# A feed-forward product of seven blocks instead of eight, in a three-product tower of layers

## The reference, cut to what matters

```python
h = s4_kernel(log_dt, x, B, inv_A_real, A_imag, 1024)      # (32, 128, 1024)
h = h + layernorm(h) @ attn_w.T + attn_b                   # 1024 x 1024
n = layernorm(h)
gates = softmax(n @ Wr.T) * 2.0                            # 4 experts
base = n @ W.T + b                                         # 1024 x 1024
lora = sum_e gates[e] * ((n @ A[e].T) @ Bm[e].T)           # rank 8 each
h = h + base + lora
```

## Time and profile before

| what | value |
|---|---|
| median of 3 runs (lowest, highest) | 809.19 us (808.93, 809.88) |
| the profiled execution: span from first to last instruction | 805.8 us |
| PE busy | 769.3 us, 95% |
| DVE busy | 622.0 us, 77% |
| ACT busy | 527.3 us, 65% |
| POOL busy | 5.5 us, 1% |
| granted TensorE clock, mean | 0.994 |
| DMA bytes | 74.65 MB |

### The profile page before, as it was taken

One profiled execution on the slowest core, in us unless ns is written; L12 is line 12 of the kernel. 1 busy time (PEld: TensorE's weight loads), 2 busy tenths in 40 slices (PEclk: granted clock), 3 DMA queues, 4 the chain that ended last, 5 costly groups with the idle time before them and its releaser, 6 DMA issues.

```text
span 805.8 us, 14896 instructions
## 1 busy us (share of the span) xinstructions
PE 769.3 (95%) x5334; PEld 377.3 (47%) x5334; DVE 622.0 (77%) x1229; ACT 527.3 (65%) x881; POOL 5.5 (1%) x22
## 2 busy tenths in 40 slices
PE   2759899999999999999999999999999999999997
PEld 1634344444444444444444444444444444444443
DVE  7899978777777787787878877777887778777532
ACT  6778876667676766766677576667766676765210
POOL 2000000000000000000000000000000000000000
PEclk9988999999999999999999999999999999999999
DMA  7869942434343333334333342434324333433323
GB/s 287 295 123 173 153 81 55 98 67 86 80 95 62 70 80 78 78 75 99 80 67 71 67 98 55 99 80 83 70 57 95 70 83 80 93 61 71 57 53 81
DMA packets 196109, 74.65 MB, mean 93 GB/s; under 512 B 184496, under 2 KB 189488, under 8 KB 195960
## 3 DMA queue, kind: packets, MB, share of 16 engines
q1 hardware_dynamic: 195992, 74.26, 42.8%
q10 hardware_dynamic: 96, 0.13, 0.0%
HBM read 14.06 MB, written 16.78 MB: 38 GB/s over the span
## 4 chain that ended last, share of the span: by engine, by line
PE 86%; DVE 4%; SPq 4%; ACT 2%; DMA 2%; issue 1%; ACTq 0%
PE ps_g L531 39%; PE ps_g L591 37%; PE ps_a L522 5%; PE ps_g L597 2%; PE ps_g L697 1%; PE ps_p L579 1%; SPq L378 1%; SPq L361 1%; DMA x<-in_L_attn_weight 1%; DVE wa_lo L1238 1%; DMA x<-x_tok 1%; PE ps_p L581 1%; ACT phase L736 0%; SPq L437 0%; DMA x<-stage 0%
## 5 line engine op out<-in xcount | busy, mean ns | idle before, releaser
L531 PE MATMUL ps_g<-wa_hi,x 128*128 128x512 f16 x1024 | 271.6, 381 | 8.3 <-DMA wa_lo<-h_tok 7.2
L591 PE MATMUL ps_g<-wf_hi,x 128*128 128x512 f16 x992 | 261.0, 379 | 0.2 <-DMA wf_lo<-stage 0.2
L531 PEld LDWEIGHTS ps_g<-wa_hi,x 128*128 128x128 f16 x1024 | 98.0, 98 | 130.6 <-issue 16.2
L531 PE MATMUL ps_g<-wa_lo,x 128*128 128x512 f16 x512 | 154.5, 381 | 0.0
L591 PE MATMUL ps_g<-wf_lo,x 128*128 128x512 f16 x496 | 148.8, 379 | 0.0
L591 PEld LDWEIGHTS ps_g<-wf_hi,x 128*128 128x128 f16 x992 | 94.9, 98 | 110.7 <-DMA wf_lo<-stage 0.7
L1198 DVE SCALAR_TENSOR_TENSOR result<-ps_g,unscale,h_tok 128x1024 f32<-128x1024 f32 x31 | 39.8, 1284 | 88.2 <-PE ps_g L597 88.2
L768 ACT ACTIVATE junk<-ps_a,stat 128x1024 bf16<-128x1024 f32 x32 | 35.2, 1101 | 68.8 <-DVE stat L1105 68.8
L531 PEld LDWEIGHTS ps_g<-wa_lo,x 128*128 128x128 f16 x512 | 50.2, 98 | 60.6 <-issue 0.8
L591 PEld LDWEIGHTS ps_g<-wf_lo,x 128*128 128x128 f16 x496 | 48.5, 98 | 58.3
L774 ACT ACTIVATE junk<-h_tok,stat 128x1024 bf16<-128x1024 f32 x32 | 36.8, 1149 | 52.2 <-DVE stat L1145 52.2
(11 more groups left out here) (214 smaller groups left out, 881.4 us busy)
## 6 DMA issues: line engine op xcount, KB each, us to landing
out<-result SPq DMA_DIRECT2D x124, 128.0 KB, 2.2
stage<-in_L_ffn_W SPq DMA_DIRECT2D x8, 512.0 KB, 14.1
x_raw<-in_x SPq DMA_DIRECT2D x38, 64.0 KB
wf_hi<-in_x SPq DMA_DIRECT2D x1, 2048.0 KB, 9.1
h_tok<-in_L_attn_weight SPq DMA_DIRECT2D x2, 512.0 KB, 4.1
x<-in_L_attn_weight SPq DMA_DIRECT2D x2, 512.0 KB, 8.1
result<-in_L_attn_weight SPq DMA_DIRECT2D x2, 512.0 KB, 9.5
x<-x_tok SPq DMA_TRANSPOSE x64, 3.2
```

The source lines that it names most:

```text
L531: mm = pe.matmul(ps[:, o, :], x1_part(part, ps is ps_g2)[:, k, :], ws[:, k, o * HALF:(o + 1) * HALF], start=k == 0 and part == 0 and ws is ...
L591: pe.matmul(ps_g2[:, o, :], xs[:, k, :], ws[:, k, o * HALF:(o + 1) * HALF], start=k == 0 and xs is x2_hi and ws is wf_hi, stop=False)
```

## The change

The two sub-tiles of a tile together are a 2 x 2 arrangement: rows are the sub-tiles (A1, A2), and columns the two halves of the 1024 input features. The weights too are cut in four blocks of 512 x 512. From tile 2 on (`FIRST = 2`) the feed-forward product of a tile is made by Winograd's form with seven block products of 128 x 512 by 512 x 512 where eight stood. Its operands are A11, A12, A22 and the sums S1 = A21 + A22, S2 = S1 - A11, S3 = A22 - S2, S4 = A12 - S2, with the weight sums T1 to T4. Tiles 0 and 1 are as before. The rest of the kernel (prologue, s4, attention product) is unchanged.

- PE: `add_form` is 12 matmuls of 512 columns; seven of them and four LoRA matmuls make a tile. Partial products stay in a bank and the next one is added on top, after DVE has read what stands there. `project_pair` makes the projections of both sub-tiles at once, in as many matmuls as before, and waits for A11, A12, S1 and A22.
- DVE: eight `take`s of 128 x 512 where two `finish`es of 128 x 1024 stood; `low_first` (128 x 1024) and five `low_form`s (128 x 512) where two `low_2`s stood; gates for both sub-tiles in one set of instructions (9 for 16).
- ACT: `high_first` and five `high_form`s where two `high_2`s stood.
- GpSimd: the four sums of each tile (`add_forms`, 128 x 512, f32), and before that 16 differences of weight blocks (`sum_weights`).
- SP: seven form transposes of a tile where four x2 transposes stood; one LoRA transpose where two stood.
- During tiles 1 and 2 the feed-forward weights are loaded again in four groups (2 x 512 KB each), subtracted by GpSimd, split by ACT and DVE (`high_sums`, `low_sums`) and turned by 16 DMA transposes.

DVE, one of the eight takes, and the order of a tile:

```diff
+            def take(t, bank, place, made, order):
+                dve.wait_ge(s_product, EACH * (t - FIRST) + made)
+                at_least(dve, s_taken, EACH * (t - FIRST) + order)
+                dve.scalar_tensor_tensor(out=place, in0=bank, scalar=unscale[:, 1:2], in1=place, op0=ALU.mult,
+                                         op1=ALU.add).then_inc(s_taken, 1)
...
+            def next_h(T, i, t, k, following):
+                keep_h(T, i)
                 if following:
+                    make_m(t + 1, k)
+                normalise_1(T, i)
                 if following:
+                    round_turns(t + 1, k)
+                low_1(T, i)
                 if following:
+                    low_m(t + 1, k)
...
+            def pair_step(t, p, ended=True, following=True):
+                if ended:
+                    keep_h(t, 1)
+                    end_22(t - 2, p)
+                    if following:
+                        make_m(t + 1, 0)
+                    normalise_1(t, 1)
+                    if following:
+                        round_turns(t + 1, 0)
+                    low_1(t, 1)
+                    if following:
+                        low_m(t + 1, 0)
+                else:
+                    next_h(t, 1, t, 0, following)
+                keep_h2(t, 0, p)
                 if following:
+                    make_u(t + 1, 0)
+                pair_gate_begin(t - 1)
+                normalise_2(t, 0, p)
+                take_p1(t - 1, 1 - p)
+                pair_gate_end(t - 1)
                 if following:
+                    low_u(t + 1, 0)
+                low_first(t)
+                take_p5(t - 1, 1 - p)
+                take_p6(t - 1, 1 - p)
+                if following:
+                    next_h(t + 1, 0, t, 1, True)
+                keep_h2(t, 1, p)
+                if following:
+                    make_u(t + 1, 1)
+                end_11(t - 1, 1 - p)
+                normalise_2(t, 1, p)
+                end_12(t - 1, 1 - p)
+                low_form(t, A22, 2)
+                low_form(t, S1, 3)
+                take_p7(t - 1, 1 - p)
+                low_form(t, S2, 4)
+                if following:
+                    low_u(t + 1, 1)
+                low_form(t, S4, 5)
+                low_form(t, S3, 6)
+                end_21(t - 1, 1 - p)
```

PE, the order of a tile:

```diff
+            def second_products(t):
+                tau = t - FIRST
+                pe.wait_ge(s_pair_t, 16 * tau + 16)
+                add_lora(bank_b, 0, 0).then_inc(s_product, 1)
+                pe.wait_ge(s_form_t[S4], 16 * tau + 16)
+                pe.wait_ge(s_taken, EACH * tau + 2)
+                add_form(bank_c, S4, plain(1, 1), False)
+                add_lora(bank_c, 0, 1).then_inc(s_product, 1)
+                pe.wait_ge(s_form_t[S3], 16 * tau + 16)
+                pe.wait_ge(s_taken, EACH * tau + 3)
+                add_form(bank_a, S3, added(T3), False).then_inc(s_product, 1)
+                pe.wait_ge(s_form_t[A22], 16 * tau + 16)
+                pe.wait_ge(s_taken, EACH * tau + 4)
+                add_form(bank_b, A22, added(T4), True)
+                add_lora(bank_b, 1, 0).then_inc(s_product, 1)
...
+            def pair_step(t, ended=True):
+                s4(t, 1)
+                if ended:
+                    last_lora(t - 2)
+                attn(t, 0)
+                project_pair(t - 1)
+                product_1(t - 1)
+                product_2(t - 1)
+                product_5(t - 1)
+                product_6(t - 1)
+                if not isinstance(t, int) or t < TILES - 1:
+                    s4(t + 1, 0)
+                attn(t, 1)
+                second_products(t - 1)
```

ACT, the second half of a tile and what follows it:

```diff
+            def second_half(t, p, waves=True, sums=False):
+                if waves:
+                    square_1(t + 1, 0)
+                    rstd_guess(t + 1, 0, stat_1, s_ssq1, s_log1, s_y1, m_eps)
+                    high_m(t + 1, 1)
+                    high_1(t + 1, 0)
+                    sines(t + 1, 1)
+                if sums:
+                    high_sums(3)
+                square_2(t, 1, p)
+                rstd_guess(t, 1, stat_2, s_ssq2, s_log2, s_y2)
+                high_form(t, A22, 0)
+                high_form(t, S1, 1)
+                high_form(t, S2, 2)
+                if waves:
+                    high_u(t + 1, 1)
+                high_form(t, S4, 3)
+                high_form(t, S3, 4)
...
+            def pair_step(t, p):
+                first_half(t, p)
                 waves_ahead(t + 1, 1)
+                second_half(t, p)
                 split_x(t + 2)
                 waves_ahead(t + 2, 0)
                 join_x(t + 2)
```

GpSimd:

```diff
+            def add_forms(t):
+                tau = t - FIRST
+                pool.wait_ge(s_xn2, 2 * t + 2)
+                if isinstance(t, int) and t == FIRST:
+                    pool.wait_ge(s_sum_t, 256)
+                else:
+                    pool.wait_ge(s_form_lo, LOWERED * tau + 1)
+                pool.tensor_tensor(form_sum[:, :], xn_b[:, 0:HALF], xn_b[:, HALF:L], ALU.add).then_inc(s_form, 1)
+                pool.wait_ge(s_form, 4 * tau + 1)
+                pool.tensor_tensor(xn_b[:, 0:HALF], form_sum[:, :], xn[:, 0:HALF], ALU.subtract).then_inc(s_form, 1)
+                pool.wait_ge(s_form_lo, LOWERED * tau + 1)
+                pool.wait_ge(s_form, 4 * tau + 2)
+                pool.tensor_tensor(xn[:, HALF:L], xn[:, HALF:L], xn_b[:, 0:HALF], ALU.subtract).then_inc(s_form, 1)
+                pool.tensor_tensor(xn[:, 0:HALF], xn_b[:, HALF:L], xn_b[:, 0:HALF], ALU.subtract).then_inc(s_form, 1)
```

SP:

```diff
+            def turn_second_forms(t):
+                turn_form(t, S1, 3, 2)
+                turn_form(t, S2, 4, 3)
+                turn_form(t, S4, 5, 5)
+                turn_form(t, S3, 6, 6)
+                turn_form(t, A22, 2, 7)
...
+            def step(t, p, stored=True, loads=True, turns=True):
+                if turns:
                     turn_x(t + 1)
+                if stored:
+                    store_pair(t - 2, 1, p)
+                if loads:
+                    load_x(t + 2)
+                turn_x1(t, 1)
+                turn_pair_lora(t - 1)
+                turn_first_forms(t)
+                if turns:
+                    turn_x1(t + 1, 0)
+                store_pair(t - 1, 0, 1 - p)
+                turn_second_forms(t)
```

More of the change, by code:

```diff
@@ L61 @@
 LORA_POWER = 2.0 ** 16
+FIRST = 2
+A11, A12, S1, S2, S4, S3, A22 = range(7)
+FORMS = 7
+EACH = 8
+LOWERED = 6
+T1, T3, T2, T4 = range(4)
 def at_least(engine, semaphore, value):
@@ L1443, in step @@
                 keep_h(*n)
+                make_m(t + 1, i)
+                normalise_1(*n)
+                round_turns(t + 1, i)
+                low_1(*n)
+                low_m(t + 1, i)
+                keep_h2(t, i, t % 2)
+                make_u(t + 1, i)
+                gate_begin(*b)
+                normalise_2(t, i, t % 2)
+                gate_end(*b)
+                low_u(t + 1, i)
+                low_2(t, i)
+            def next_h(T, i, t, k, following):
+                keep_h(T, i)
@@ new lines, in _ @@
+            make_u(3, 1)
+            low_sums(3)
+            normalise_2(2, 1, 0)
+            low_form(2, A22, 2)
+            low_form(2, S1, 3)
+            low_form(2, S2, 4)
+            low_u(3, 1)
+            low_form(2, S4, 5)
+            low_form(2, S3, 6)
+            pair_step(3, 1, ended=False)
+            with dve.Fori(2, TILES // 2 - 1) as two:
+                pair_step(2 * two, 0)
+                pair_step(2 * two + 1, 1)
+            pair_step(TILES - 2, 0)
+            t = TILES - 1
@@ L1480 @@
+            pair_step(t, 1, following=False)
+            end_22(t - 1, 0)
+            take_p1(t, 1)
+            pair_gate_begin(t)
+            pair_gate_end(t)
+            take_p5(t, 1)
+            take_p6(t, 1)
+            end_11(t, 1)
+            end_12(t, 1)
+            take_p7(t, 1)
+            end_21(t, 1)
+            end_22(t, 1)
 _INS = ["x", "L0_tok_log_dt", "L0_tok_B", "L0_tok_inv_A_real", "L0_tok_A_imag", "L0_attn_weight",
```

525 lines of the change are left out of this document (412 added, 113 removed).

## The result

The changed kernel takes 902.83 us (median of 4, 902.2 to 904.9) against 809.06 us (4 runs of the kernel before beside it, 808.67 to 809.88): a ratio of 1.117, 95% interval 1.1151 to 1.1189. The forecast was 870 us, 836 to 902: the direction came true, the size did not, and the result lies 0.8 us above the range.

A forecast was written before the change was run, and what follows sets the result against it. PE was taken as the bound, DVE next; afterwards DVE's cycle would set the tile. 12 periods 33.6, GpSimd beside DVE 3.6, switch-over 12.9 and end 10.7 made +60.8 us: 870 us against 809.19, range 836 to 902.

The forecast's parts named there:

- PE gains 2.6 us a tile: PE: twelve matmuls of 0.216 us fewer in a tile, a period of 43.7 us if everything else keeps up.
- DVE's work, 41.9 us: DVE per tile: 38.2 us before plus 3.7 (takes +3.0, low forms +1.9, gates -1.2).
- The turned x, 4.6 us: make_m: x's transpose behind S3's and A22's takes 7.6 us, DVE fills 3.0, so waits 4.6 every tile.
- The chain of the sums, 2.4 us: DVE's waits per tile: S1 0.65, high_u 0.35, ACT's half of S3 0.65, ACT's square of h2 0.7.
- GpSimd beside DVE, 0.3 us a tile: Loss of DVE's two-input form halves beside GpSimd sums: 0.3 us a tile, bounds 0 and 2.2.
- The two-input row: Two 64-column scalar_tensor_tensors on DVE: 0.55 us beside GpSimd, 0.49 away from it; taken as a small loss.
- The row of 9.93: A 64-column DVE tensor_scalar starting at 9.93 took 0.51 us, ending just after the GpSimd instruction; cited for the full lock.
- Rival 1: Full lock beside GpSimd: 2.2 instead of 0.3 us a tile, 7 us more at the switch-over, 900 us; chance 0.17.
- a tile: DVE's sum per tile: 41.9 + 4.6 + 2.4 = 48.9 us, 49.1 with handover, against 46.3 before.
- Switch-over, 12.9 us: At tile 2, once: +10.4 us with a PE wait of about 17 us, plus 2.5 for the clock after it.
- The end, 10.7 us: From attention (15, 0) to the last DVE instruction: 66.7 us against 56.0, PE waits of 4.4, 1.1 and 0.9 included.
- What the profile would show: Right: make_m wait 4 to 5 us, periods near 49.4, long PE wait; wrong: period below 46, no wait, halves above 0.75.

The follow-up runs named there:

- e12: e11 with the switch-over reordered as in e8: 832.5 us, ratio 1.030 to the kernel before.
- e2: The changed kernel with GpSimd's four sums made on one column instead of 512 from the fourth tile on: 894.66 us, ratio 1.110.
- e1: The changed kernel with x split by ACT ahead of its square of h2 and turned by SP ahead of the second form transposes: 896.37 us, ratio 1.109.
- e3: The changed kernel with the edits of e1 and e2 together: 851.68 us, ratio 1.053.
- e7: e1 with the four sums of a tile made by DVE instead of GpSimd from the fourth tile on: 903.14 us, ratio 1.118.
- e13: e10 with S3's halves in a place of their own, sums still on GpSimd: 852.7 us, ratio 1.054.
- e9: The changed kernel with u of the next tile split ahead of the second-half forms on ACT and DVE: 935.8 us, ratio 1.157.
- e6: e1 with 34 matmuls of 256 columns, whose result nothing reads, ahead of s4(t,1): 872.73 us, ratio 1.080.
- e8: The changed kernel with x of tile 3 ahead of the second group of weight sums and groups three and four one place earlier: 898.04 us, ratio 1.111.
- e10: The changed kernel with e9's order and e1's early x, sums still on GpSimd: 873.53 us, ratio 1.081.
- e11: e10 with the four sums on DVE and S3's halves in a place of their own: 839.0 us, ratio 1.038.
- e14: e10 with the four sums on DVE, S3's halves still in S1's place: 872.8 us, ratio 1.079.
- e4: The kernel before plus eight GpSimd sums of 128 x 512 a tile on a buffer that nothing reads: 811.41 us, ratio 1.004.
- e5: The changed kernel with 34 matmuls of 256 columns, whose result nothing reads, ahead of s4(t,1): 906.25 us, ratio 1.121.

## Why the prediction was wrong

Of the 34.8 us by which the span misses (+95.6 for +60.8) 18.0 lie in the 12 tiles, 10.2 in the switch-over, 5.4 at the end and 1.2 ahead of tile 2. Point by point, by its own steps.

**PE gains 2.6 us a tile.** Right: 46.30 - 43.78 = 2.5 in e12. In the changed kernel PE is busy 45.8 us a tile (458.26 over ten), because some 2 of the 2.5 go to matmuls at the lower clock.

**DVE's work, 41.9 us.** Right but for the lock. Of the 43.2 us busy in a tile 2.9 are the lock (e2), which leaves 40.3, 3.6 over before's 36.7; the step had +3.7.

**The turned x, 4.6 us.** Right: 4.4 us in each of 11 waits, and e1, which puts x early, makes it vanish.

**The chain of the sums, 2.4 us.** With the handover of 0.2 it was 2.6 us of waits beside x's. Measured are 1.6, and they are for PE; the chain's own waits are covered by the lengthened halves. Its third part, ACT's half of S3 waiting for S1's place, was put at 0.65 us. With the lock gone it is 1.8 us a tile (e2), with x's wait gone too 3.0 and 4.2 (e3, e7), and freeing the place is worth 20.8 us in e13.

**GpSimd beside DVE, 0.3 us a tile: this is the step that failed.** The prediction had both readings and took the wrong one. It is 2.9 us a tile (e2 against after), above even the 2.2 that the Trainium skill's rule gave in it (SBUF — State Buffer, Who interferes with whom: the loser of the shared port pair is blocked for the whole instruction). The trace agrees with that rule in its kind: instructions with two SBUF inputs are lengthened, takes from PSUM are not. The size was larger than the 2.2 because four instructions are held, not two: low_u for 1.1 us of the 2.9 and three halves for 1.9; and the sums take 1.27 us and up to 1.71 beside DVE, not 1.15. The two-input row that decided for 0.3 was misread. It ran from 9.35 to 9.90, and the GpSimd instruction of 256 columns began at 9.78: they stood side by side for 0.12 us only. The row of 9.93, which did stand beside it, showed the block. Rival 1, with the lock in full, gave 900 us against 902.8 measured, and its sign in the profile, halves longer than 0.75 us beside GpSimd, is there. That its total comes so near is in part luck: it had nothing more for the end, where 5.4 us were missing, and 23 us for the tiles, where 18.0 were.

With the measured prices DVE's list closes: 49.4 us, 2.6 more for the lock, 1.0 less for the chain and 0.2 less for x are 50.8 a tile, as measured. What the list can't tell is what a cure is worth: e2, which takes the lock away, gains 0.7 us a tile, not 2.9. The prediction's sum of **a tile** lacked the second cycle: it added up DVE's list and let PE wait beside it for nothing. PE's waits of 3 to 6 us bring the clock down, s4 then takes 2.75 for 1.49 (after) and a product 5.30 for 2.75 (e2, e9), and those microseconds stand in the cycle through attention, norm, forms and low_u, which e1 shows at 50.4 us without x's wait and without changing the lock. e6, which only keeps PE busy, takes 2 us a tile off it.

**Switch-over, 12.9 us.** It was 23.1. The layout had one wait of PE of about 17 us, which was 20.3; it had not the other, 10.9 us for the LoRA transpose of tile 1. DVE's gates for that transpose stand behind its wait of 10.75 us for x of tile 3 (it ends at 160.38), which the layout did not have either; in e8 that wait falls to 2.3, and the weight sums that were moved up stand there in its place.

**The end, 10.7 us.** It was 16.1. PE's three waits were foreseen about right in sum (4.21 for the first product, 1.11 for a take and 0.42 for the LoRA transpose, together 5.7 for 6.4), but not the clock behind them: the 24 matmuls at 873.05 take 8.02 us where the chain has 5.19 for as many at full clock, and attention 10.87 for 10.47. That is 3.2 us of the 5.4. Another 0.8 lie in the stores behind DVE's last instruction (3.6 us for 2.8); the rest is open.

**What the profile would show.** The wait at make_m of 4 to 5 us, low_u and a take as what PE waits for, DVE's waits for PE nearly gone, and a long PE wait around 200 us are all there; the period of 49.4 is not, and of the signs of being wrong the long halves are.

What stays open: how much of the switch-over the LoRA wait alone costs, and how the lock, the place and the clock share the 4.5 us a tile in the changed kernel itself. Single edits don't split them there, since taking away the lock or x's wait alone gains 0.7 us or less and the fill nothing; the place alone was not tried there. The steps of e10, e13, e11, in that order, are one path only, and e14 shows that another order gives other shares.

## What to carry to other kernels

When work is taken off the bounding engine and put on another, write down every cycle that then comes near the bound, each with its waits and its lower-clock stretches, and not only the busiest engine's list: here three of 50 to 51 us hid one another, two edits gave 6.5 and 8.2 us alone and 51 together, and one cost 33 us alone and gave 23 beside another. Sums put on GpSimd are not free beside VectorE instructions with two SBUF inputs, and a stage that only pays back 2.5 us a tile must be run over enough tiles to cover its start and its end. Before a row is taken as the price of standing beside another engine, work out from both starts and durations how long the two really overlapped: here it was 0.12 us.

## What the runs showed of the hardware that was not expected

- A GpSimd sum of 128 x 512 (1.27 us alone) lengthens VectorE's two-input instructions of 512 columns from 0.69 to between 1.1 and 1.75 us and those of 1024 from 1.22 to 2.28, and is itself lengthened to between 1.6 and 2.1. An instruction with two SBUF inputs that starts as a sum ends keeps its 1.21 us, and the next sum takes 2.00 for 1.04 (e4). In e4 a cast of 64 columns with a single input was held as well, 0.20 to 0.51 us on the mean, while keep_h, keep_h2 and finish, which read PSUM, kept their 1.28. The Trainium skill (SBUF — State Buffer, Who interferes with whom) names, beside two SBUF inputs, VectorE's two-port modes as holders of the pair; the cast's row agrees with that, if it ran in one, which no row tells.
- Behind a wait of PE of 3.3 to 6 us the granted clock was at the lower of its two levels (1.2 GHz, 0.50): 12 matmuls took 5.30 us for 2.75, s4 2.75 for 1.49 (2.11 and 2.40 in two of 13 tiles). Behind waits of 1.66 us (e12) the full clock stayed (1.00). In e5 it went both ways: 12 matmuls took 2.76 us behind a wait of 2.38 and 4.43 behind one of 2.31.
- Matmuls whose result nothing reads, put in such a wait, made a kernel 2.6% faster (e6 against e1), but only where the cycle through PE was the bound (e5 against after: none).
